# Two cross attentions over masked keys regrouped into quads of heads: four score banks, two projection banks, one transpose bank

## What is computed

```
q = layernorm(x) @ Wq * 64**-0.5                 # 16 heads of 64
k, v = split(context @ Wkv)                      # 375 keys a head
sim  = q @ k.T ; sim[masked keys] = min_float
out  = softmax(sim) @ v
x    = x + tanh(gate) * (out @ Wo) ; then a gelu MLP
```

## Time and profile before

| | us |
|---|---|
| median of 3 runs | 2025.97 |
| their lowest and highest | 2022.82, 2027.89 |
| the profiled execution's own time | 2026.49 |
| span of that execution in the trace | 2024.5 |
| TensorE busy, of the span | 1915.1 (95%) |
| VectorE, ScalarE, GpSimd busy | 1131.6, 831.1, 883.7 |
| mean granted TensorE clock, of full speed | 0.980 |

### The profile page before, as it was taken

One profiled execution on the slowest core, in us unless ns is written; L12 is line 12 of the kernel. 1 busy time (PEld: TensorE's weight loads), 2 busy tenths in 40 slices (PEclk: granted clock), 3 DMA queues, 4 the chain that ended last, 5 costly groups with the idle time before them and its releaser, 6 DMA issues.

```text
span 2024.5 us, 35457 instructions
## 1 busy us (share of the span) xinstructions
PE 1915.1 (95%) x12620; PEld 1643.0 (81%) x12620; DVE 1131.6 (56%) x2699; ACT 831.1 (41%) x2198; POOL 883.7 (44%) x1037
## 2 busy tenths in 40 slices
PE   4999989997999999999999999998979999999998
PEld 3776777776999989888988879985458988888997
DVE  6777866665543654547676554222384766655422
ACT  2017527884211211256666423222235666652321
POOL 3340313240888999642121338850044212104884
PEclk9999988998999999999999999999989999999999
DMA  3110100010333333310000123322221000001332
GB/s 127 42 58 2 40 16 17 30 54 3 96 113 106 114 114 115 98 35 18 10 24 12 55 76 105 105 83 88 76 75 35 18 10 24 13 1 42 105 115 78
DMA packets 38189, 118.87 MB, mean 59 GB/s; under 512 B 6168, under 2 KB 10264, under 8 KB 38016
## 3 DMA queue, kind: packets, MB, share of 16 engines
q1 hardware_dynamic: 31408, 107.92, 17.2%
q10 hardware_dynamic: 6608, 8.68, 1.4%
HBM read 114.75 MB, written 1.84 MB: 58 GB/s over the span
## 4 chain that ended last, share of the span: by engine, by line
PE 82%; DVE 7%; POOL 5%; ACT 2%; issue 2%; DMA 1%; DVEq 0%; ACTq 0%; SPq 0%; POOLq 0%
PE psum L580 15%; PE psum L582 14%; PE psum L581 14%; PE psum L802 7%; PE psum L813 6%; PE psum L860 5%; PE psum L573 4%; PE psum L700 4%; PE psum L702 4%; PE psum L701 4%; POOL wl L1760 3%; ACT probs_t L1067 1%; POOL wh L1752 1%; PE psum L874 1%; DVE rstd L1316 1%
## 5 line engine op out<-in xcount | busy, mean ns | idle before, releaser
L1760 POOL TENSOR_TENSOR wl<-raw,wh 128x256 fp32r<-128x256 f32 x656 | 512.5, 812 | 13.7
L1752 POOL TENSOR_SCALAR wh<-raw 128x1024 fp32r<-128x1024 f32 x164 | 189.5, 1155 | 402.0 <-PE psum L582 161.1
L580 PE MATMUL psum<-nh,wh 128*128 128x448 f32 x904 | 349.6, 387 | 14.2 <-DVEq L1531 5.3
L581 PE MATMUL psum<-nl,wh 128*128 128x448 f32 x904 | 337.0, 373 | 0.0
L582 PE MATMUL psum<-nh,wl 128*128 128x448 f32 x904 | 336.7, 372 | 0.0
L1067 ACT ACTIVATE probs_t<-masked_t,nmin 112x375 f32<-112x375 f32 (+1 forms) x384 | 202.6, 528 | 109.7 <-DVE nmin L1434 109.7
L1607 DVE TENSOR_TENSOR hid_l<-scr,hid_h 128x448 fp32r<-128x448 f32 x108 | 92.3, 855 | 227.7 <-ACT hid_h L1153 227.1
L580 PEld LDWEIGHTS psum<-nh,wh 128*128 128x128 f32 x904 | 175.0, 194 | 37.1 <-issue 13.3
L1434 DVE CUSTOM_DVE_ANT_0 masked_t<-psum,maskf 112x375 f32<-112x375 f32 x256 | 129.8, 545 | 116.6 <-PE psum L802 116.0
L1094 ACT COPY probsT_t<-psum 125x336 f32<-125x336 f32 (+1 forms) x424 | 175.4, 456 | 43.5 <-PE psum L860 24.3
L813 PE MATMUL psum<-cst,probs_t 112*125 112x112 f32 (+1 forms) x1304 | 189.7, 276 | 3.6 <-ACT probsT_t L1094 3.2
(11 more groups left out here) (192 smaller groups left out, 3874.1 us busy)
## 6 DMA issues: line engine op xcount, KB each, us to landing
raw<-in_walls SPq DMA_DIRECT2D x183, 512.0 KB, 3.6
raw<-in_ctxF SPq DMA_DIRECT2D x24, 375.0 KB, 3.0
ctxb<-in_ctxF ACTq DMA_DIRECT2D x8, 375.0 KB, 3.5
ctxt<-in_ctxK ACTq DMA_DIRECT2D x8, 375.0 KB
x<-in_xT ACTq DMA_DIRECT2D x2, 896.0 KB, 11.5
outT<-x SPq DMA_DIRECT2D x2, 896.0 KB, 5.1
mask<-in_kmask ACTq DMA_DIRECT2D x16, 41.0 KB, 2.6
vself<-in_tt SPq DMA_DIRECT2D x1, 448.0 KB, 6.8
```

Source lines behind the costliest of these rows:

```text
L580: nc.tensor.matmul(out, ah, bh, start=(i == 0), stop=False)
L581: nc.tensor.matmul(out, ah, bl, start=False, stop=False)
L1752: nc.gpsimd.tensor_scalar(high, src, 1.0, 1.0, ALU.mult, ALU.mult).then_inc(split_h, 1)
L1760: last = nc.gpsimd.tensor_tensor(low[cut], src[cut], high[cut].bitcast(F32), ALU.subtract)
```

## The change

The two keyed attentions leave `attention` for a function `keyed` on each engine that works quad by quad; the other attentions keep `attention`. Bank 5 goes from the transposes to the projections, which then use 0 and 5; banks 1 and 2 go to the scores, and all transposes of a keyed attention go to bank 6. The third slot for keys is dropped, NPROB grows from 6 to 8.

```diff
-NPROB = 6
+NPROB = 8
...
-        self.k_slots = 3 if mask == "keys" else 2
+        self.k_slots = 2
...
-        self.s_banks = 4 if mask is None and nh > 1 else 2
+        self.s_banks = 4 if k_heads else 2
...
-        kk2 = sb("kk2", [P, 2, 376], F32R)
...
-        def t_bank(g):
-            return psum[:, 5 + g % 2, :]
+        def t_bank(a, g):
+            return psum[:, 6 if a.mask == "keys" else 5 + g % 2, :]
...
-                return [("K", i, 0) for i in range(a.k_slots - 1)] + ([("V", 0, 0), ("V", 0, 1)] if second < 0 else [])
+                return [("K", 0, 0), ("V", 0, 0), ("V", 0, 1)] if a is att_c0 else [("K", 0, 0), ("K", 1, 0)]
...
-            return kk[:, i % a.k_slots] if i % a.k_slots < 2 else kk2
+            return kk[:, i % 2]
...
-                    if a is att_c0:
-                        pe.wait_ge(a.exped, s - a.s_banks + 2)
-                    else:
-                        pe.wait_ge(a.maxed, s)
+                    pe.wait_ge(a.exped if a is att_c0 else a.maxed, s - a.s_banks + 2)
...
                 pe.wait_ge(a.exped if a is att_c0 else a.scaled, s + 1)
-                if g >= 2 and s % a.group == 0:
+                if a.mask == "keys":
+                    if g >= 1:
+                        pe.wait_ge(a.probs_out, g)
+                elif g >= 2 and s % a.group == 0:
                     pe.wait_ge(a.probs_out, g - 1)
```

The new order on TensorE, and the line in the layers' loop that calls it:

```diff
+            def keyed(a):
+
+                quads, n_keys = a.steps // 4, a.steps // a.k_heads
+                for n in range(quads + 2):
+                    if n < quads:
+                        scores(a, 4 * n)
+                        scores(a, 4 * n + 2)
+                    if 0 <= n - 2:
+                        weigh(a, n - 2)
+                    for j in range(4):
+                        if j < 2 and 2 * n + 2 + j < n_keys:
+                            project(a, "K", 2 * n + 2 + j, 0)
+                        if j >= 2 and n < quads:
+                            project(a, "V", n, j - 2)
+                        if 0 <= n - 1 < quads:
+                            turn(a, 4 * n - 4 + j)
...
-                attention(a)
+                plan.use([0, 5])
+                keyed(a)
+                pe.wait_ge(a.maxed, a.steps)
+                plan.use(range(POOL))
```

The new order on ScalarE:

```diff
+            def copy_turned(a, t):
+
+                act.wait_ge(a.turned, t + 1)
+                if t >= NTURN:
+                    act.wait_ge(a.summed, (t - NTURN) // 4 + 1)
+                nc.scalar.copy(probsT[t % NTURN][0:a.kw, 0:CH * S], t_bank(a, t)[0:a.kw, 0:CH * S]).then_inc(a.probs_out, 1)
+
+            def keyed(a):
+
+                quads, n_keys = a.steps // 4, a.steps // a.k_heads
+                for n in range(quads + 1):
+                    for j in range(4):
+                        if n < quads:
+                            exponents(a, [4 * n + j])
+                        if 1 <= j < 3:
+                            if 2 * n + 1 + j < n_keys:
+                                project(a, "K", 2 * n + 1 + j, 0)
+                            if n >= 1:
+                                copy_turned(a, 4 * n - 4 + j - 1)
+                    for j in range(2):
+                        if n >= 1:
+                            copy_turned(a, 4 * n - 2 + j)
+                        if n < quads:
+                            project(a, "V", n, j)
+                    if n % 4 == 3 and n // 4 + 2 < B:
+                        context(a, n // 4 + 2)
```

The new order on VectorE:

```diff
+            def keyed(a):
+
+                dve.wait_ge(chain, link(nc.vector.memset(probs_t[:, :, S2:S2 + 1], 0.0)))
+                quads, n_keys = a.steps // 4, a.steps // a.k_heads
+                for n in range(quads + 2):
+                    if 1 <= n <= quads:
+                        own = slice(4 * (n - 1) % NPROB, 4 * (n - 1) % NPROB + 4)
+                        dve.wait_ge(a.exped, 4 * n)
+                        nc.vector.reciprocal(rinv[:, own], rsum[:, own]).then_inc(a.recip, 1)
+                        dve.wait_ge(a.recip, n)
+                        for r in range(4 * n - 4, 4 * n):
+                            pr = probs[r % NPROB][:, 0:S2 + 1]
+                            nc.vector.tensor_scalar(pr, pr, rinv[:, r % NPROB:r % NPROB + 1], None, ALU.mult)\
+                                .then_inc(a.scaled, 1)
+                    if n < quads:
+                        for t in range(4 * n, 4 * n + 4):
+                            smallest(a, t)
+                    for i in (2 * n + 2, 2 * n + 3):
+                        if i < n_keys:
+                            project(a, "K", i, 0)
+                    if n >= 2:
+                        out_group(a, n - 2)
```

More of the change, by code:

```diff
@@ L812, in turn @@
                     o = (s % a.group + c) * S
-                    last = nc.tensor.transpose(t_bank(g)[0:a.kw, o:o + S],
+                    last = nc.tensor.transpose(t_bank(a, g)[0:a.kw, o:o + S],
                                                probs[s % NPROB][:, c * a.kw:(c + 1) * a.kw], ident[0:S, 0:S])
@@ L1093, in attention @@
                         w = max(a.group, a.chunks) * S
-                        nc.scalar.copy(probsT[g % NTURN][0:a.kw, 0:w], t_bank(g)[0:a.kw, 0:w]).then_inc(a.probs_out, 1)
+                        nc.scalar.copy(probsT[g % NTURN][0:a.kw, 0:w], t_bank(a, g)[0:a.kw, 0:w]).then_inc(a.probs_out, 1)
                         if a is att_2 and 3 <= g < B - 1:
```

## The result

The changed kernel takes **2029.66 us** (median of 20 runs, 2027.89 to 2032.82), the kernel before on the same chip 2025.43 us (20 runs, 2021.35 to 2031.32). The ratio is 1.0025, with a 95% interval of 1.0018 to 1.0031: slower by about 5 us, inside the 0.3% that I had called no change, and at the far end of the range. I had forecast 2019.5. The profiled execution took 2030.16 us, its span is 2028.0 against 2024.5.

The account below looks back on a forecast made before the run. TensorE was taken to set the pace, at 8.565 us a quad. Each keyed attention was to change by -4.1 us, two by -8.2, with the clock -6.5: from median 2025.97 to 2019.5 us, range 2006 to 2032.

Parts of the forecast that it names:

- point 6: Two projection banks and key slots for three: free in steady quads; first quad waits for K's subtraction, +1.1 us an attention.
- Point 8: Clock at the ends of the keyed attentions: both expected to drop once, +1.7 us in all.
- Rival B: Both attention ends run at half clock throughout, 2.2 us more an attention than Point 8: 2024 us; chance 0.10.
- the sum without the clock: Forecast for one keyed attention before the clock's price is added: -4.1 us; two give -8.2.
- Points 1 and 2: Fewer block entries on TensorE an attention: scores of four heads together, -5.8 us; K entered once a quad, -6.4 us.
- rival D: Entries come from each block's first matmul with its waits, not the array's division: 12.8 us back, 2032; chance 0.05.
- Point 3: Weighing entered from scores instead of transposes: no difference, range -9 to +3 us over both attentions.
- Point 4: Spreading the transposes on TensorE: each still steps by 0.107 us; priced at nothing, to -0.6 us an attention.
- Point 5: One transpose bank: wait for the copy behind V part 1, +0.14 us a quad, +4.3 us an attention.
- rival A: The copy does not hold V part 1 and the clock stays up at the ends: 2007.5 us; chance 0.20.
- Point 7: Attention's end: transposes wait with nothing between, 1.17 us a round trip; idle 2.8 becomes 5.4, +2.7 us.
- Rival C: VectorE's four scalings make ScalarE and the one transpose bank late, deciding from 1.2 us a quad: 2043 us; chance 0.17.

Follow-up runs that it names:

- e2_before_hid96: Kernel before with hid_h and hid_l alone moved by 64 bytes, to place 96 modulo 256; ratio 1.0028.
- e1_before_moved: Kernel before with its third key slot placed behind the hidden tiles' region, so that these stand at 96; 2032.82 us, ratio 1.0030.
- e1_before_again: Kernel before, unchanged, timed and traced again; ratio 0.9999.
- e2_turn_first: Changed kernel with each head's transposes ahead of the projection on TensorE, and ScalarE's copies reordered to match; 2036.85 us, ratio 1.0039.
- e1_after_gap: Changed kernel with the third key slot kept in SBUF unused, hidden tiles back at 32; 2027.05 us, ratio 0.9993.
- e2_hid0: Changed kernel with hid_h and hid_l alone moved by 32 bytes, to place 128 modulo 256; ratio 0.9993.
- e3_hid192: Changed kernel with hid_h and hid_l alone moved by 192 bytes, to place 32 modulo 256; ratio 1.0001.
- e3_hid3008: Changed kernel with hid_h and hid_l alone moved by 3008 bytes, to their address in the kernel before; ratio 1.0005.
- e3_tail_gap: Changed kernel with the last quad's second and third head transposed into free score banks 3 and 4, and the third key slot kept unused; ratio 0.9951.
- e4_high96: Kernel before with hid_h at place 96 and hid_l at 32 modulo 256; ratio 1.0020.
- e4_low96: Kernel before with hid_l alone moved by 64 bytes, to place 96 modulo 256; ratio 1.0017.

## Why the prediction was wrong

**The step that failed is the one that cost nothing on paper.** That "the change touches nothing else but the number of buffers for exponentials" is false of the addresses. I had counted what the third key slot holds and who waits for it, and priced its removal at nothing outside point 6; the tiles behind it moved by 3008 bytes. Place alone costs 0.28 to 0.30%, 5.7 to 6 us (e2_before_hid96, e1_before_moved). The steps of the two profiled executions say the same within what they vary by: 1515 steps of 1.5 ns more and twice 738 of 3.6 more are 7.6 us.

**Point 8 was too small.** I let the lower clock end with the attention. At attention 3 the fall cost 1.4 us inside the attention (273.4 against the 272.0 of attention 1, which kept its clock in both executions of the changed kernel) and 2.4 in Wo behind it (44.7 against 42.3 before): 3.8, where I had put 1.7 on an end. The 1.7 was not all clock either: in e1_before_again attention 1 kept its clock and took 276.1, still 0.5 more than attention 3, so the fall before had cost 1.2. The lower level was granted within Wo at 14 of the 16 ends of the eight profiled executions with the new regrouping and the old end (e2_turn_first among them), and Wo then took 43.6 to 45.3 us; at none of the 12 ends with the old order (42.3 to 42.8); and at 2 of the 8 with the repaired end, though these two waited no longer than the other six. What decides there is open. Rival B had the right idea at attention 3, and stopped at the attention too.

**One more stretch got longer without being touched**, the one between the first keyed layer's MLP and attention 3. Busy time by stretch, kernel before, then changed kernel (granted clock is the third number from the end):

```profile
1361.00:1537.60 176.60, 153.86 (x563) 101.67 (x561) 75.37 (x114) 51.35 (x94) 40.28 (x45) 0.94 0.23 74
```

```profile
1357.00:1538.07 181.07, 157.14 (x563) 102.53 (x561) 75.21 (x114) 51.36 (x94) 40.84 (x45) 0.92 0.22 72
```

The same 563 matmuls, between many waits of TensorE, with a granted clock of 0.92 instead of 0.94. Over all profiled executions this stretch averages 178.1 us with the old order (6 executions, 176.5 to 180.0; one of them at 0.92) and 180.3 with the new one (12, 177.3 to 182.0; ten of them at 0.92 or 0.93). That the order is behind it is read from these averages alone; what it would do to the clock there was not tested.

**The sum closes on average, to some 2 us.** The changed kernel against the one before: attentions -6.8 to -7.5, Wo +2.1 to +2.5, the stretch at 0.92 +2.2, the MLPs +5.7: about +3, with 2.4 and 5.1 measured. With the place no longer 96: attentions -6.2, Wo +3.6 (88.4 for both, the mean of e1_after_gap, e2_hid0, e3_hid192 and e3_hid3008, against 84.8), the stretch +2.2: -0.4, with ratios of 0.9993, 1.0001 and 1.0005 measured at place 32. Both sums leave out what lies ahead of the first attention, whose start varied from 875.8 to 880.6 us with the old order and from 873.2 to 879.1 with the new. In the first profiled pair it came 2.4 earlier, though the first MLP lies there: attentions -7.5, Wo +2.5, the stretch +4.4, the MLPs of layers 1 and 3 +6.5 and this -2.4 make the 3.5 by which the span grew. The order's own gain in the attentions is thus real and spent again: on Wo, where the lower clock is seen, and in the stretch, where the clock is the likely cause but was not tested; the place then makes the kernel slower.

**What was right.** The attentions gave 6.8 to 7.5 us against 6.5 forecast, a steady quad 8.34 against 8.33; with the clock up at its end, attention 1 went from 276.1 (e1_before_again) to 272.0, 4.1 as in the sum without the clock. Points 1 and 2: the scores of four heads add 1.21 (forecast 1.20), and K is entered dearly once a quad; rival D is dead, since a first K behind transposes adds 0.19. Point 3: the weighing stands behind scores and adds 1.30 as it did behind transposes, so that pairing costs what the others do. The Trainium skill (TensorEngine Tiling (Array Packing), Key Properties) says that each change of tiling mode drains the engine. The trace agrees as far as it shows: K's first matmul adds 0.37 behind a weighing and 0.19 behind transposes. Point 4: three transposes step by 0.107. Point 5: the wait is 0.13, forecast 0.14, so rival A fell. Point 6: in steady quads TensorE waits neither for K's subtraction nor for the second transpose; in the first quads it waits for K's subtraction, 1.8 us in all against 2.2 forecast, as this group of TensorE's instructions has it (busy, mean ns of one, idle before, releaser):

```profile
L579 PE MATMUL psum<-kvwh,ctxh 128*125 128x256 f32 x384 | 117.8, 307 | 1.8 <-DVE kk L1449 1.8
```

Point 7: the bank's round trips at the end are 1.17 each, as said.

**Rival C** did not come in the changed kernel: 24 quads are all TensorE. How near it is, I may have misjudged. I gave 1.2 us of lateness as the point from which it decides; in e2_turn_first, with the quad shorter by 0.13 and ScalarE's order changed, one quad of four is past it. Why one in four is read from the chain alone and was not tried: VectorE casts a new mask once in four quads, and the cast stands in the long one. The Trainium skill (TensorEngine Tiling (Array Packing), PSUM Bottleneck) warns of copies out of PSUM as the bound. In e2_turn_first the trace agrees only in part: TensorE waits for ScalarE's copy (2.9 us in five waits between 925 and 1125), but what makes that copy late is the scalings, the cast and the exponentials ahead of it.

## What to carry to other kernels

Where a change drops or resizes a buffer, write down the addresses of all that lie behind it, before and after, and give their readers a price; or keep the hole until the rest is timed, as e1_after_gap does with one line. Where a chain of short waits is added just ahead of dense matmuls, the clock's price can be paid in the matmuls behind it, as at 14 of 16 ends here: measure until the step is back at its fast value, not until the stage ends. And give an end without cover its own banks: with both repairs this kernel is 10 to 13 us faster than the one before, where the regrouping alone gave none.

## What was not expected of the hardware

- TensorE's step for matmuls of 448 columns, all at full clock and with no wait, depended on where their operand lies within 256 bytes: about 205.3 ns (205.1 to 205.7, six executions of five kernels, all three MLPs) at 96; 202.8 to 204.0 at 128; 203.8 to 204.7 at 160; 203.2 at 0; 201.4 to 203.8 at 32, with one MLP of one kernel (e3_tail_gap) at 206.1. The places at 0, 128 and 160 had one kernel each.
- At 32 the step is not one number: one program had 201.6 in an MLP of one execution and 203.6 in the same MLP of another. What switches it is open, as is why the place counts at all.
- The matmuls of these MLPs that read nh and nl, which did not move, stepped more slowly as well when both hidden tiles stood at 96: in the third MLP 206.2 ns in e2_before_hid96 against 202.5 in the kernel before, and 202.5 and 202.6 with only one of the tiles there (e4_high96, e4_low96). The writes of the hidden tiles by VectorE or ScalarE could be behind it rather than TensorE's own reads; no run told these apart.
